# Value projection of six groups by seven block products ahead of the attention, scores two heads ahead, and the scaling of probabilities moved to GpSimd

## The reference

```
x = x + tanh(g_xattn) * xattn(layernorm(x), ctx, mask)
x = x + tanh(g_ffn)   * moe(layernorm(x))

xattn(h, c, mask):                       # 32 heads of 128
    q = rmsnorm(h) @ w_q.T;  k = c @ w_k.T;  v = c @ w_v.T
    s = softmax(mask(q k^T + position_bias[head]))        # per head and sequence
    return h + (s @ v) @ w_out.T
```

## Time and profile before

| what | value |
|---|---|
| median of 3 runs | 987.17 us (986.87 to 989.12) |
| profiled execution: time | 987.9 us |
| profiled execution: span | 986.2 us |
| TensorE busy | 957.9 us, 97% |
| VectorE busy | 622.7 us, 63% |
| ScalarE busy | 402.8 us, 41% |
| GpSimd busy | 256.3 us, 26% |
| DMA, mean over the span | 162 GB/s |

### The profile page before, as it was taken

One profiled execution on the slowest core, in us unless ns is written; L12 is line 12 of the kernel. 1 busy time (PEld: TensorE's weight loads), 2 busy tenths in 40 slices (PEclk: granted clock), 3 DMA queues, 4 the chain that ended last, 5 costly groups with the idle time before them and its releaser, 6 DMA issues.

```text
span 986.2 us, 13781 instructions
## 1 busy us (share of the span) xinstructions
PE 957.9 (97%) x4915; PEld 798.6 (81%) x4915; DVE 622.7 (63%) x996; ACT 402.8 (41%) x1006; POOL 256.3 (26%) x242
## 2 busy tenths in 40 slices
PE   6999999999999999999999999999999999999994
PEld 5888888888888888888888888888888877777772
DVE  6877669667655357666755667556675597843321
ACT  5336554333332355353452534525345244324442
POOL 1353334343432112110111101101011002053364
PEclk9999999999999999999999999999999999999997
DMA  6645454666665334132331323313233239565589
GB/s 250 222 175 203 170 201 154 224 227 224 210 219 181 142 134 165 60 134 88 134 118 62 134 89 134 119 61 134 89 134 121 100 136 362 184 228 176 172 188 240
DMA packets 68627, 160.20 MB, mean 162 GB/s; under 512 B 7728, under 2 KB 28464, under 8 KB 66384
## 3 DMA queue, kind: packets, MB, share of 16 engines
q1 hardware_dynamic: 61008, 143.99, 40.9%
q0 software_dynamic: 4784, 12.58, 5.5%
q10 hardware_dynamic: 2768, 2.75, 0.8%
HBM read 104.97 MB, written 54.33 MB: 162 GB/s over the span
## 4 chain that ended last, share of the span: by engine, by line
PE 71%; DVE 5%; DMA 2%; ACT 2%; issue 1%; POOL 1%; SPq 0%; DVEq 0%; ACTq 0%
PE ps_job L673 11%; PE ps_job L675 11%; PE ps_job L674 11%; PE ps_score L810 6%; PE ps_attn L838 5%; PE ps_attn L1068 5%; PE ps_turn L824 3%; PE ps_job L1077 2%; PE ps_attn L715 1%; PE ps_attn L716 1%; PE ps_attn L717 1%; DMA y_slots<-y_out 1%; PE ps_turn L1052 1%; PE ps_score L715 1%; DMA w_raw<-wa_dram 1%
## 5 line engine op out<-in xcount | busy, mean ns | idle before, releaser
L597 POOL TENSOR_TENSOR score_bias<-mask_bias,pos_bias 128x1024 f32<-128x1024 f32 x32 | 76.8, 2399 | 394.5 <-DVE probs L1537 378.4
L1123 ACT ACTIVATE probs<-probs,neg_max 128x128 f32<-128x128 f32 x256 | 99.4, 392 | 71.4 <-DVE neg_max L1540 71.4
L673 PE MATMUL ps_job<-wv_hi,ctx_lo 128*128 128x512 f32 x256 | 101.1, 395 | 0.0
L675 PE MATMUL ps_job<-wv_hi,ctx_hi 128*128 128x512 f32 x256 | 99.8, 390 | 0.0
L674 PE MATMUL ps_job<-wv_lo,ctx_hi 128*128 128x512 f32 x256 | 99.7, 389 | 0.0
L1537 DVE TENSOR_TENSOR probs<-ps_score,score_bias 128x512 f32<-128x512 f32 x64 | 43.9, 685 | 74.8 <-PE ps_score L810 70.6
L1113 ACT ACTIVATE pT<-ps_turn 128x512 f32<-128x512 f32 x64 | 35.1, 596 | 118.3 <-PE ps_turn L824 118.3
L1113 ACT ACTIVATE v_s<-ps_job 128x512 f32<-128x512 f32 x64 | 38.2, 597 | 88.1 <-PE ps_job L675 88.1
L1563 DVE TENSOR_TENSOR acc<-ps_job,acc 128x512 f32<-128x512 f32 x56 | 38.6, 690 | 55.0 <-PE ps_job L675 54.2
L577 POOL TENSOR_TENSOR w_sum<-w_raw 128x256 f32<-128x256 f32 x30 | 24.0, 800 | 180.9 <-PE ps_score L717 69.1
L1068 PE MATMUL ps_attn<-ew_s,xbT 128*128 x248 | 62.3, 380 | 0.9 <-ACT xbT L1113 0.9
(11 more groups left out here) (406 smaller groups left out, 2328.9 us busy)
## 6 DMA issues: line engine op xcount, KB each, us to landing
kq<-st SPq DMA_DIRECT2D x32, 1024.0 KB, 4.2
kq_s<-kq SPq DMA_DIRECT2D x64, 512.0 KB, 4.5
w_raw<-wa_dram SPq DMA_DIRECT2D x31, 512.0 KB, 5.8
y_slots<-ones SPq DMA_DIRECT2D x32, 256.0 KB, 4.9
wv_raw<-wv_dram SPq DMA_DIRECT2D x8, 1024.0 KB, 5.0
ew_s<-ew_dram SPq DMA_DIRECT2D x4, 2048.0 KB, 14.2
y_slots<-y_out SPq DMA_DIRECT2D x31, 256.0 KB, 2.8
wo_raw<-wo_dram SPq DMA_DIRECT2D x7, 1024.0 KB, 4.7
```

The source lines that it names most:

```text
L597: nc.gpsimd.tensor_tensor(score_bias[:], mask_bias[:], pos_bias[:, i % 2].unsqueeze(1).broadcast_to([P, B, P]), ALU.add).then_inc(bias_rea ...
L673: nc.tensor.matmul(psum, l_lo, r_hi, start=(k == 0), stop=False)
L675: last = nc.tensor.matmul(psum, l_hi, r_hi, start=False, stop=(closed and k == n - 1))
L1123: last = nc.scalar.activation(probs[:, half, b], probs[:, half, b], ACT.Exp, bias=neg_max[:, half, b:b + 1], accum_out=row_sum[:, half, b: ...
```

## The change

1. Steps 32 to 43 are added to the projection (`KQ` = 32 steps for k and q, `PAIRS` = 3, `BH` = 4 steps each): a pair of groups' v for all eight tiles is computed in four steps of seven products, and stored to a DRAM buffer `v_all`. A pair's weights (four blocks, 2 MB in four transfers) are loaded by `load_wv`; their four sums are formed by VectorE for the first pair (`sum_wv_first`, in step 31) and by GpSimd for the others (`sum_wv`); high and low parts are spread over the steps (`high_wv`, `low_wv`).
2. v of groups 6 and 7 is made in the old way (16 tiles, `project_v(m)`) at the start of the attention: five tiles ahead of head 0, then 3, 3, 3 and 2 with heads 0 to 3. ScalarE copies each to `v_out` (two places), SyncE stores it to `v_all` (`keep_v`), and the copy of tile m waits for the store of tile m - 2.
3. `v_s` is loaded per group from `v_all` (2 MB, `load_v`).
4. Scores run two heads ahead (`score(i + 2)`); `probs`, `neg_max` and `row_sum` get a second buffer. `kq_s` keeps two.
5. The probabilities are scaled on GpSimd (`scale_rows`), head i ahead of the bias of head i + 2.
6. Later heads have two job tiles each, all of the output projection. wo gets two buffers.
7. At the end VectorE takes the low part of head 31 ahead of the residual adds; `out_part(t, [G - 2])` of all four tiles follows `attend(H - 1)`.

```diff
+KQ = H
+PAIRS = NG // 2 - 1
+STEPS = KQ + BH * PAIRS
+ORDER = (A11, S2, S1, S3, A12, S4, A22)
+AHEAD = range(5)
+FILL = (range(5, 8), range(8, 11), range(11, 14), range(14, 16))
...
+            def load_wv(u):
+                for r in range(2):
+                    for d in range(2):
+                        block = ((A11, A12), (S3, A22))[r][d]
+                        sp.dma_start(v_raw[u % 2][block][:], wv[2 * u + r][:, HALF_C * d:HALF_C * (d + 1)])\
+                          .then_inc(wv_in, 16)
...
+            def keep_v(m):
+                sp.wait_ge(v_sbuf, m + 1)
+                sp.dma_start(v_all[2 * PAIRS + m // B, m % B], v_out[:, m % 2]).then_inc(v_kept[m % 2], 16)
...
+                if s == KQ - 2:
+                    sp.wait_ge(a_psum, prod(s, 7))
+                    load_wv(0)
...
+            for u in range(PAIRS):
+                for n in range(BH):
+                    if n == 0 and u + 1 < PAIRS:
+                        sp.wait_ge(a_psum, prod(v_step(u, 0) - 1, 7))
+                        sp.wait_ge(wv_split, 7 * (u + 1))
+                        load_wv(u + 1)
...
+                    store_v(u, n)
             sp.wait_ge(a_psum, prod(STEPS - 1, 7))
-            sp.dma_start(wv1_raw[:], wv[1]).then_inc(wv_in, 16)
+            load_v(0)
+            sp.wait_ge(wv_last_split, 1)
+            load_wv_last(1)
+            load_wo(0)
             for i in range(H):
...
+                if i == 1:
+                    load_v(1)
+                if i < G:
+                    for m in (AHEAD, FILL[0], FILL[1], FILL[2])[i]:
+                        keep_v(m)
+                if i == G:
+                    for m in FILL[3]:
+                        keep_v(m)
+                if j == 0 and g:
+                    if g + 1 < NG:
+                        sp.wait_ge(attn_psum, 2 * i)
+                        load_v(g + 1)
+                    if g == 1:
+                        sp.wait_ge(v_psum, 2 * B)
+                    else:
+                        sp.wait_ge(o_psum, B * (g - 1))
+                    load_wo(g)
                 if i == H - G:
                     sp.dma_start(x_res[:], x.rearrange("t p d -> p t d")).then_inc(x_res_in, 16)
...
+            bias_scores(0)                      # GpSimd
+            bias_scores(1)
+            scale_rows(0)
+            bias_scores(2)
+            for i in range(1, H):
+                scale_rows(i)
+                if i + 2 < H:
+                    bias_scores(i + 2)
...
             score(0)                            # TensorE
-            for t in range(B):
-                project_v(0, t)
+            for m in AHEAD[:-2]:
+                project_v(m)
+            score(1)
+            for m in AHEAD[-2:]:
+                project_v(m)
             for i in range(H - 2):
                 g, j = divmod(i, G)
                 turn_probs(i)
-                score(i + 1)
+                score(i + 2)
                 attend(i)
...
+            def take_v(m):                      # ScalarE
+                act.wait_ge(v_psum, m + 1)
+                if m >= 2:
+                    act.wait_ge(v_kept[m % 2], 16 * (m // 2))
+                copy(v_out[:, m % 2], ps_job[m % 2][:]).then_inc(v_sbuf, 1)
...
+            for m in AHEAD:
+                take_v(m)
+                if m in (1, 3):
+                    exps(0, m // 2)
+            exps(1, 0)
+            for i in range(H):
+                g = i // G
+                if i == 0:
+                    exps(1, 1)
                 take_pT(i)
...
+            def low_wv(u, k):                   # VectorE
+                block = ORDER[k]
+                dve.wait_ge(wv_summed, 4 * (u + 1))
+                dve.wait_ge(wv_hi_done, 7 * u + k + 1)
+                V.tensor_tensor(v_lo[u % 2][block][:], v_raw[u % 2][block][:], hi_of(u, k)[:], ALU.subtract)\
+                 .then_inc(wv_split, 1)
...
+                if s == KQ - 1:                 # after the fourth product's add
+                    sum_wv_first()
+                    low_wv(0, 0)
...
+                    if u + 1 < PAIRS:           # same place, steps n = 0 to 3 of pair u
+                        for k in ((), (0,), (1,), (3,))[n]:
+                            low_wv(u + 1, k)
...
-                V.tensor_tensor(probs[:, half], probs[:, half],
-                                row_scale[:, half].unsqueeze(2).broadcast_to([P, BH, P]),
-                                ALU.mult).then_inc(probs_ready, 1)
```

More of the change, by code:

```diff
@@ L61 @@
 T_ORDER = (T1, T3, T2, T4)
+ORDER = (A11, S2, S1, S3, A12, S4, A22)
+HI_PLACES = 10
 def prod(s, n):
@@ L460, in load_pos, with load_v @@
                 sp.dma_start(pos_bias[:, i % 2], pbias[i]).then_inc(pos_in[i % 2], 16)
+            def load_v(g):
+                if g < 2 * PAIRS:
+                    for n in range(BH - 2, BH):
+                        s = v_step(g // 2, n)
+                        sp.wait_ge(kq_stored[s % 2], stores(s))
+                else:
+                    for n in range(2):
+                        sp.wait_ge(v_kept[n], 16 * B)
+                if g:
+                    sp.wait_ge(v_in, 16 * g)
+                sp.dma_start(v_s[g % 2][:], v_all[g].rearrange("t p k -> p t k")).then_inc(v_in, 16)
@@ L509, in _ @@
             sp.wait_ge(residual_added, B)
-            for n in range(0, E, E // 4):
-                if n == E - E // 4:
+            for n in (4, 8, 12, 0):
+                if n == 0:
                     sp.wait_ge(o_psum, B * NG)
@@ L590, in _, with bias_scores @@
                     to_minus_half(rms[:], rms[:], 2)
+            for u in range(1, PAIRS):
+                sum_wv(u)
             pool.wait_ge(mask_done, 1)
             pool.wait_ge(a_dve, dve_took(STEPS - 1, 5))
-            for i in range(H):
+            def bias_scores(i):
                 pool.wait_ge(pos_in[i % 2], 16 * (i // 2 + 1))
@@ L844, in _ @@
             pe.wait_ge(ident_done, 2)
-            for s in range(NPLAIN, STEPS):
+            for s in range(NPLAIN, KQ):
                 project_seven(s)
@@ L907, in _ @@
             pe.wait_ge(attn_split, 2 * (H - 2))
+            for t in (2, 3):
+                out_ahead(t)
+            turn_probs(H - 1)
+            for t in (0, 1):
+                out_ahead(t)
+            attend(H - 1)
+            pe.wait_ge(attn_split, 2 * (H - 1))
             for t in range(4):
-                out_ahead(t)
-            pe.wait_ge(attn_split, 2 * (H - 1))
-            for t in range(2):
                 out_part(t, [G - 2])
-            turn_probs(H - 1)
-            out_part(2, [G - 2])
-            attend(H - 1)
-            out_part(3, [G - 2])
             pe.wait_ge(attn_split, 2 * H - 1)
```

503 lines of the change are left out of this document (304 added, 199 removed).

## The result

The changed kernel takes 1021.98 us (median of 4, 1019.81 to 1023.34) against 987.02 us (median of 4) for the kernel before on the same chip: ratio 1.0348, 95% interval 1.0321 to 1.0375. The sign was as forecast, but 1022 lies above the range of 990 to 1018: the loss is 35 us where 20 were forecast. The profiled execution took 1020.68 us, its span 1018.9, so 32.7 more than the span before.

What follows compares the result with a forecast made beforehand. TensorE, busy 957.9 of 986.2 us, was taken as the bound. Savings of 16.3 and 1.8 us against new waits and clock losses summed to +20.2, from 987.2 to 1007.4 us, with 990 to 1018 for 8 in 10.

Steps and rivals of the forecast that it cites:

- Forecast A: Whole kernel: transfers queue, new waits of about 38 us outweigh 18.1 saved; own range 997 to 1017 us, chance 0.75.
- the 16.3 us: Computing v on TensorE: 504 matmuls in place of 576, 72 fewer at 0.2267 us each, -16.3 us.
- The 1.8 us of group 0: Group 0's heads: scores two heads ahead free them of 4 x 0.44 us lost between heads, -1.8 us.
- Entering v: Step 32 waits for the first wv pair's landing, then VectorE's sums and splits: +11.0 us (10 to 12.5).
- B: Rival: only the small stores and k, q are not delayed; +2.0 us, 989 us, about no change; chance 0.09.
- C: Rival: transfers don't delay each other at all, so the kernel gets faster; -9 us, 978 us; chance 0.07.
- D: Rival: GpSimd's scalings and the port lock make two-tile heads some 11.5 us rather than 9.9; 1050 us; chance 0.04.
- the step on the clock: Long new waits of TensorE halve its clock, up to 2.4 us each: +1.5 us of a possible 9.6.
- the later pairs: Second and third wv pairs: loads land after 7.2 us, then sums; stalls of 3.5 and 3.1 us, +6.6 us.
- k and q of head 7: Queued behind large loads, they land 15.0 us after R (head 4's start on TensorE), scores due at 10.8: +4.2 us.
- The entry: From v into attention: tile 0's store queues behind loads until T + 21.1 (T: last v step's end); +9.9 us.
- The tail: Kernel end: residual adds now follow head 31's attn_lo, first output add 1.8 us later; +1.8 us (0 to 2.5).

Runs made afterwards that it cites:

- scale_dve: Changed kernel with the scaling of the probabilities back on VectorE, GpSimd keeping the bias alone: 1023.47 us, ratio 1.0351 to the kernel before.
- clock_fill: Changed kernel with matmuls whose results nothing reads added in five waits of TensorE, no wait removed: 1013.53 us, ratio 1.0266 to the kernel before.
- combo3_fill: combo3 with 33 matmuls whose results nothing reads in the wait ahead of step 32: 986.71 us, ratio 0.9990 to the kernel before.
- combo4_fill: combo4 with 33 matmuls whose results nothing reads in the wait ahead of step 32: 983.95 us, ratio 0.9952 to the kernel before.
- wv_early: Changed kernel with the next pair's wv loaded once the running pair's four sums are made, not all seven splits: 1009.79 us, ratio 1.0207.
- kq_ahead: Changed kernel with loads of v, wo and x issued one head later, behind k and q of the group's last head: 1009.81 us, ratio 1.0221.
- wv_alone: Changed kernel with the store of a pair's first step issued only when the next pair's weights have landed: 1022.44 us, ratio 1.0343.
- combo4: combo3 with VectorE's split of the last wv moved behind head 0's attn_lo: 983.66 us, ratio 0.9945 to the kernel before.
- keep_act: Changed kernel with the 0.25 MB stores of kept v tiles issued from ScalarE's queue, not SyncE's: 1009.67 us, ratio 1.0214.
- combo: Changed kernel with wv_early, kq_ahead and a new SyncE order at the attention's entry, k and q of head 2 first: 990.15 us, ratio 1.0017.
- combo3: combo with ScalarE taking head 0's turned probabilities ahead of v tile 4, and v of group 1 loaded at head 2: 988.15 us, ratio 1.0006.
- combo2: combo with kept tiles stored from ScalarE's queue and large loads spread over heads 0 to 2: 993.49 us, ratio 1.0043 to the kernel before.

## Why the prediction was right or wrong

**Right.** Forecast A's mechanism and its places: transfers queue, and each wait that it named was there, released by what it named. The 9.52 us of a step held for the twelve v steps, so the 16.3 us were won; group 0's heads lost nothing to each other. (The 1.8 us of group 0 were counted from one pair of heads: in the kernel before three heads, and not four, were 0.44 too long, but head 4 was by 0.5.) Entering v was 11.5 for 11.0, idle 8.46 for "about 8", and its causes, the landing of the weights (VectorE's first sum starts at 326.0, forecast 325.0) and VectorE's 17 us behind it, are what no experiment moved: they are read from the trace alone. Rivals B and C fell with the result; D fell with the 9.9 us between heads and with scale_dve. Neither engine is a bound for the scaling.

**Wrong: the step on the clock.** "Most are followed by work that waits on other engines anyway: +1.5 of a possible 9.6." They are not. Behind five of the six waits comes TensorE's own work with its operands ready (twelve matmuls of v twice, a tile, sixteen scores twice), and it was done at 1.2 GHz: 8.8 us by the trace, 8.5 by clock_fill. Only entering v hides it: nine matmuls 0.43 apart cost 1.9 us there, but TensorE then waits 0.65 us for `v_lo` all the same, and combo3_fill and combo4_fill got 0.1 and 0.3 back. (The hiding is not complete: in wv_early, kq_ahead and scale_dve 12 to 14 matmuls were at half rate there, and the step was about 1 us longer.) The prediction had the price per wait in hand (2.4 at most, 1.6 to 2.1 measured) and multiplied it by the wrong number of waits; the sum with it would have been 1014.7. Of the 12.4 us that the sum missed, 7.3 are this term, 4.1 the later pairs and 1.9 head 5; the others cancel to 0.9 the other way. The Trainium skill (TensorE: Matmul & The Clock Gate, What's actually happening) has idleness put the array on half rate; the trace agrees at all six waits (the granted clock is 0.50 to 0.66 behind each), the one of 2.4 us at head 29 among them.

**Too small: "4.2 + 3.0 = 7.2" for a pair's load.** This was the cost that was mis-sized. It was 10.5 and 9.45, and GpSimd and VectorE follow it step by step, so the stalls were 5.8 and 4.6 (with the half rate behind them 7.7 and 6.4) for 3.5 and 3.1. The first of these loads on SyncE, and GpSimd's first sum behind it:

```profile
342.89 1.84 SPq L504 DMA_DIRECT2D v_raw<-wv_dram  x4
```
```profile
353.39 2.40 POOL L680 TENSOR_TENSOR v_raw<-v_raw,v_raw 128x1024 f32<-128x1024 f32 x1 [44.79 <-DMA v_raw<-wv_dram]
```

What is issued behind shares the engines (1.0 us of it, by wv_alone); the rest is that 2 MB of loads took 8.5 to 9.6 us even with nothing behind, and 8.7 as one transfer.

**Too small: k and q of head 7,** 6.0 us of wait for 4.2. The landing at R + 15.0 took SyncE to be free at R + 1.0 and counted 4.25 MB. The large loads were issued from R + 1.3 on, and k and q of head 8, issued 1.8 us behind those of head 7, are one more MB in flight with them, which the prediction left out: they landed at R + 17.0. That this MB is the reason is argued; no run moved it. SyncE's issues there (v, k and q of head 7, k and q of head 8):

```profile
541.72 0.37 SPq L529 DMA_DIRECT2D v_s<-v_all  x1
...
542.94 1.19 SPq L514 DMA_DIRECT2D kq_s<-kq  x2
...
544.78 1.48 SPq L514 DMA_DIRECT2D kq_s<-kq  x2
```

**The entry,** 12.0 for 9.9: 1.7 are the clock. The chain was right (ScalarE's copy of tile 2 waited for the store of tile 0 and began at T + 22.2, forecast T + 21.1) but it wasn't the only one: the store of tile 0, k and q of head 2, ScalarE's order and VectorE's order each became the late one as soon as the one ahead of it was mended, and only all these moves together (combo4) brought 12.0 down to 0.9. ScalarE's wait in the changed kernel:

```profile
485.56 1.22 ACT L1270 ACTIVATE v_out<-ps_job 128x512 f32<-128x512 f32 x2 [12.59 <-DMA v_all<-v_out]
```

**The tail,** +0.7 for 1.8: counted from head 30's turning and less the 9.1 us of work that changed sides, the first output add comes 1.9 us later, as described, and TensorE waits 2.01 us for it. The half rate behind this wait costs nothing, since VectorE sets the pace there, 1.85 us a tile as before. Where the other 1.2 us are made up stays open.

**The range.** Its upper end of 1018 rested on "ends rarely meet". Even all upper ends together gave only +33, which is 1020 and still under 1022. (By its own terms the entry's upper end should be 12.0, 9.9 and 5.3 x 0.4, and not 11.5; and the sum of the lower ends takes 2.5, 2.5 and 1 where the terms name 0.) The clock term met in all places because one mechanism sets it: errors that share a cause add up, and belong at one end together.

## What to carry to other kernels

A new wait of TensorE costs its length and then the half rate of the work behind it, 1.6 to 2.1 us here for waits of 2.4 to 8.2 us; leave that out only where the work behind waits on another engine anyway. The arithmetic saving of this change was real from the start (18 us), and of the 50.7 us of losses some 36 were the order of issue and of the engines' programs (12.8 of the later pairs, 12.5 of heads 5 and 29, 11.1 of the entry, in combo4); the 11.5 of entering v stayed: before judging such a change, ask for each small transfer that something waits for what megabytes are issued ahead of it, and for each engine what stands in its program behind a wait that is not urgent. When one wait is mended look at once for the next, since on a path of several engines the first mend may return a quarter of the loss: the entry went from 12.0 to 9.0 (keep_act), 6.0 (combo), 5.3 (combo3) and, with the last move, to 0.9.

## What the runs showed of the hardware

- Even the wait of 2.01 us at the end of the changed kernel's attention is followed by matmuls 0.43 us apart:

```profile
841.00 0.48 PE L1038 MATMUL ps_job<-wo_hi,attn_lo 128*128 128x512 f32 x1 [2.01 <-DVE acc L1840]
841.30 0.60 PE L1039 MATMUL ps_job<-wo_lo,attn_hi 128*128 128x512 f32 x1
841.70 0.63 PE L1040 MATMUL ps_job<-wo_hi,attn_hi 128*128 128x512 f32 x1
```

- Matmuls whose results nothing reads, put into a wait, kept the granted clock at 1.00 where waits of 2.4 to 8.5 us had been, and saved 8.5 us.
- A 256 KB store landed in 2.1 us (median of tiles 5 to 15 of the changed kernel) with nothing large issued just ahead of it, and in 6.5 to 6.6 on ScalarE's own queue (keep_act, combo2) while large loads on SyncE's kept the DMA engines busy, at some 400 GB/s in all.
- A single load of 2 MB landed in 8.7 us, four of 512 KB in 8.5 and 9.6 with nothing behind them.
- GpSimd multiplied 128x512 by a broadcast row factor in 1.04 us, less than half of the 2.40 of its 128x1024 add.
